# One graph layer's edge tiles on one core: which edges of part one go into the tile that both sorted parts share

## The reference

```python
edge_index = jnp.stack([src, dst])                 # sorted by dst
h = jnp.maximum(_layernorm(x, axis=-1), 0.0)
x = x + _L0_gnn_ref(h, edge_index, W, b)            # degree-normalised sum over edges, then a linear layer and relu
h = jnp.maximum(_layernorm(x, axis=-1), 0.0)
x = x + _L1_gnn_ref(h, edge_index, Wq, ...)

def _L1_gnn_ref(node_embeds, edge_index, ...):
    rows, cols = edge_index                         # rows = src, cols = dst
    q = node_embeds[rows] @ Wq.T + bq
    k, v = node_embeds[cols] @ Wk.T + bk, node_embeds[cols] @ Wv.T + bv      # 8 heads of 16
    exp_att = exp(clip(sum(q * k, per head) / 4, -10, 10))
    out = segment_sum(exp_att / (segment_sum(exp_att, rows)[rows] + 1e-8) * v, rows)
    return layernorm(out + node_embeds) * gamma + beta
```

## Time and profile before

| what | us |
|---|---|
| executions, lowest, median, highest | 2271.06, 2272.73, 2276.27 |
| profiled execution, span from first to last instruction | 2940.6 |
| setup and first tiles, 0 to 230 of the span | 230 |
| edge loop of the first layer, 230 to 1450 | 1220 |
| node rows and list of tiles, 1450 to 1575 | 125 |
| passes, 1575 to 2884 | 1309 |
| end | 56 |

### The profile page before, as it was taken

One profiled execution on the slowest core, in us unless ns is written; L12 is line 12 of the kernel. 1 busy time (PEld: TensorE's weight loads), 2 busy tenths in 40 slices (PEclk: granted clock), 3 DMA queues, 4 the chain that ended last, 5 costly groups with the idle time before them and its releaser, 6 DMA issues. The chain is left out here.

```text
span 2940.6 us, 44304 instructions
## 1 busy us (share of the span) xinstructions
PE 1840.2 (63%) x10257; PEld 1461.4 (50%) x10258; DVE 1874.7 (64%) x5089; ACT 1279.6 (44%) x3362; POOL 1551.0 (53%) x1594
## 2 busy tenths in 40 slices
PE   5323346767576676677776767676666676666662
PEld 4323334544344444344454656566556665656662
DVE  9858775655455755455775666666666666666666
ACT  8524345755465565556653323333223332322333
POOL 0256655665556565565434555545455555555544
PEclk7756667877778787878887888888888888888886
DMA  3211111111111111111116444445444544444453
GB/s 105 62 41 42 43 39 39 45 42 38 38 38 45 38 41 41 39 44 39 33 68 185 126 125 127 127 122 131 119 121 124 132 123 122 125 123 123 126 122 55
DMA packets 234145, 244.06 MB, mean 83 GB/s; under 512 B 32925, under 2 KB 195229, under 8 KB 233989
## 3 DMA queue, kind: packets, MB, share of 16 engines
q0 software_dynamic: 61136, 147.00, 18.5%
q1 hardware_dynamic: 142357, 81.55, 10.8%
q10 hardware_dynamic: 30624, 15.21, 2.2%
HBM read 225.01 MB, written 18.62 MB: 83 GB/s over the span
## 5 line engine op out<-in xcount | busy, mean ns | idle before, releaser
L303 POOL DMA_INDIRECT rows<-y_tab,idx x832 | 795.6, 956 | 589.8 <-issue 307.9
L1340 POOL DMA_INDIRECT x<-kv_tab,kv_idx x672 | 682.7, 1016 | 623.0 <-DVE msg L1392 403.9
L1563 PE MATMUL ps_kv<-kv_s,hot_low 128*128 x1362 | 406.0, 443 | 168.9 <-DVE hot_low L1364 90.0
L780 ACT ACTIVATE sort_v<-sort_t,staged,minus 128x128 f16<-128x128 f16 x914 | 360.7, 480 | 309.1 <-remote 243.1
L872 PE MATMUL ps_sort<-sort_hi,sort_v 128*128 128x496 f16 x1662 | 417.6, 403 | 117.3 <-issue 112.4
L619 DVE TENSOR_SCALAR sort_v<-iota_h,staged 128x128 f16<-128x128 f16 x748 | 243.2, 325 | 339.2 <-remote 269.0
L1550 PE MATMUL ps_m<-msg,x 128*128 128x136 f32 x1792 | 295.4, 315 | 243.4 <-DVE msg L1392 182.7
L830 PE MATMUL ps_sum<-rows,hot 128*128 128x128 f32 x1664 | 282.0, 323 | 250.3 <-issue 120.1
L1374 DVE TENSOR_TENSOR by_tile<-ps_q,x 128x512 f32<-128x512 f32 x224 | 154.5, 690 | 404.9 <-remote 257.4
L830 PEld LDWEIGHTS ps_sum<-rows,hot 128*128 128x128 f32 x1664 | 260.4, 235 | 271.8 <-issue 139.4
L1550 PEld LDWEIGHTS ps_m<-msg,x 128*128 128x128 f32 x1792 | 263.3, 219 | 263.1 <-issue 245.7
(11 more groups left out here) (290 smaller groups left out, 2072.2 us busy)
## 6 DMA issues: line engine op xcount, KB each, us to landing
weights<-tile_tab SPq DMA_DIRECT2D x114, 256.0 KB
x<-tile_tab SPq DMA_DIRECT2D x113, 256.0 KB
weights<-tile_tab ACTq DMA_DIRECT2D x58, 256.0 KB
rows<-y_tab,idx POOLq DMA_INDIRECT x832
x<-kv_tab,kv_idx POOLq DMA_INDIRECT x672
kv_tab<-kv_s SPq DMA_DIRECT2D x12, 512.0 KB
x<-x_in SPq DMA_DIRECT2D x1, 3328.0 KB, 13.3
out<-x SPq DMA_DIRECT2D x12, 256.0 KB
```

The costliest lines, as they stand in the source:

```text
L303: pool.indirect_dma_start(out=rows[:, k * SPAN + n, :], out_offset=None, in_=y_tab, in_offset=bass.IndirectOffsetOnAxis(ap=idx[:, k, n:n + ...
L780: last = nc.scalar.activation(to[:, k % 2, m, :], sort_t[:, k % 2, m, :], ACT.Relu, bias=staged[:, v, c:c + 1], scale=minus[:, v, c:c + 1])
L1340: pool.indirect_dma_start(out=rows[:, u, k, :], out_offset=None, in_=kv_tab, in_offset=bass.IndirectOffsetOnAxis(ap=idx[:, u, k:k + 1], ax ...
L1563: last = nc.tensor.matmul(ps_kv[:, k % 2, :], hot_low[:, w, k * P:(k + 1) * P], kv_s[:, ds(low + w, 1), :], start=w == 0, stop=w == WINDOW ...
```

## The change

It changes which `low` edges of part one go to the shared tile: the last ones instead of the first. Part one's whole tiles come first in the numbering and the shared tile last (so the high part of part one's numbers now names the block's first tile plus its t0 div 128 whole tiles), the lane isn't mirrored any more, and the column of part one's tiles is computed with NB instead of NB - 1. The number of tiles and of edges in each stays as it was. Three prefetches behind SP's loop of passes get another form of wait, which bounds the register's value from below and adds a no-operation.

```diff
@@ -440,15 +440,17 @@
                 then(nc.vector.tensor_copy(tiles[:, :, :], tiles_i[:, :, :]))
+                then(nc.vector.tensor_scalar(count[:, 0, :], tiles[:, 0, :], float(2 ** LIN), None, ALU.mult))
                 then(nc.vector.tensor_tensor_scan(flat(tend), flat(tiles), zeros_h[:, 0:2 * NB], 0.0, ALU.add, ALU.add))
...
-                nc.vector.tensor_scalar(count[:, 0, :], low, -1.0, float(P - 1), ALU.mult, ALU.add)
+                then(nc.vector.tensor_scalar(tiles[:, :, :], tiles[:, :, :], float(2 ** LIN + P), -float(MID * 2 ** LIN), ALU.mult, ALU.add))
+                then(nc.vector.tensor_tensor(tiles[:, 0, :], tiles[:, 0, :], count[:, 0, :], ALU.add))
+                nc.vector.memset(count[:, 0, :], -1.0)
                 then(nc.vector.tensor_scalar(count[:, 1, :], low, -1.0, None, ALU.add))
-                then(nc.vector.tensor_scalar(tiles[:, :, :], tiles[:, :, :], float(2 ** LIN + P), -float(MID * 2 ** LIN), ALU.mult, ALU.add))
                 then(nc.vector.tensor_tensor(tiles[:, :, :], tiles[:, :, :], count[:, :, :], ALU.add))
@@ -568,15 +570,16 @@
-                nc.vector.tensor_scalar(run[:, PARTS[0]], lane_of[:, PARTS[0]], -1.0, float(P - 1), ALU.mult, ALU.add)
-                nc.vector.tensor_copy(run[:, PARTS[1]], lane_of[:, PARTS[1]])
+                nc.vector.tensor_copy(run, lane_of)
...
-                then(nc.vector.scalar_tensor_tensor(out=pos, in0=tile_f, scalar=float(NB - 1), in1=sbk[:, :], op0=ALU.add, op1=ALU.subtract))
+                for part in range(2):
+                    then(nc.vector.scalar_tensor_tensor(out=pos[:, PARTS[part]], in0=tile_f[:, PARTS[part]], scalar=float(NB - part),
+                                                        in1=sbk[:, PARTS[part]], op0=ALU.add, op1=ALU.subtract))
@@ -1314,9 +1317,9 @@
-                def load_src(i, u):
+                def load_src(i, u, after=sp.wait_ge):
 
-                    sp.wait_ge(off_made, i * QUADS + u + 1)
+                    after(off_made, i * QUADS + u + 1)
@@ -1326,7 +1329,7 @@
                 for u in range(QUADS - 1):
-                    load_src(passes, u)
+                    load_src(passes, u, lambda semaphore, value: wait_positive(sp, semaphore, value))
```

## The result

The changed kernel takes 2239.12 us (median of 4, 2236.35 to 2244.36) beside 2274.50 for the kernel before (median of 4, 2271.06 to 2277.89): a ratio of 0.9851, interval 0.9834 to 0.9868, or 35.4 us less. The forecast was 2238 us.

A forecast was written before the change was run, and what follows sets the result against it. The prediction took a ring of DVE and PE to bound the passes, 23.2 us each when profiled. Two passes at 17.9 us saved 35.8, additions cost 0.5: 2272.7 - 35.3 = 2237.4, said as 2238 us; range 2225 to 2250.

The forecast's parts named there:

- The count: Tiles counted on the reference's inputs: narrow 184 to 206, fetched 670 to 648, so passes of the loop 56 to 54.
- The price of a pass: Stage 4's loop: a pass without the profiler takes 17.9 us, so two passes fewer save 35.8 us.
- the factor 0.773: Median 2272.73 us over the profiled span; scaled a pass from 23.2 to 17.9 us, the surplus laid to the profiler.
- The bounds: A pass's price lies between 15.3 us, four quads of the fastest stretch, and 23.2 us, the profiled mean.
- The ring of DVE and PE: Stage 4's passes: expand, products, scores, exponential, values, sums, next quad bound a pass; 23.2 us, DVE's own work 14.9.
- rival 1: Every pass runs like the fastest stretch, 15.3 us; 2242.6 us, chance 0.24; against it, POOL's 12 gathers already take 15.1.
- the weighed rule: Slow clock belongs to an idle TensorE; without the profiler PE stays nearer full clock and a pass costs the dense stretch's price.
- The additions: DVE's extra instructions in setup and behind the ranks: 0.65 us, taken as exposed, bounds 0 and 1.3.
- SP's waits: Three new-form waits behind SP's loop of passes: taken as 0, with 0.5 us at most.
- Dense passes: Without the profiler every pass runs like the fastest stretch, 15.3 us; 2242.6 us, chance 0.24.
- Dear passes: Surplus lies in stages 1 to 3, so a pass keeps 23.2 us; 2226.8 us, chance 0.06.
- The other three: 55 passes, 2255.3 us (0.04); timed inputs not those counted, about 2273 (0.02); slower instruction supply in passes, 2282 (0.04).

The follow-up runs named there:

- Narrow_of_two: Changed kernel with a narrow tile's limit set to a difference of 1 block instead of 2; 3160.40 us on chip B, 1.0743 of before.
- after: The changed kernel's own profiled execution, of the short kind, 2242.7 us long.
- after_again: The changed kernel itself, run again on chip C beside the kernel before; 2886.54 us, 0.9822 of before.
- waits_alone: Kernel before with only SP's three bounded waits added, on chip A; 2277.74 us beside 2277.71 for before, ratio 0.9996.
- nine_gathers_b: Changed kernel with three gathers in each fetched quad instead of four, on chip C; 2677.34 us, 209 us less than the changed kernel there.

## Why the prediction was right, point by point

**The count.** 854 tiles, 206 narrow, 648 fetched, 54 passes: shown by 648 gathers and 216 products. That there was no tile to spare did no harm. Narrow_of_two confirmed the method with 780 gathers. That most of the gain comes from part one's whole tiles and not from the shared ones is the count's statement, which the reference's inputs give again; no run separates the two, since they are one choice.

**The price of a pass.** The sum took 17.9 us, the runs show 16.65 (33.3 us for two, 35.8 forecast). It came out near because the factor 0.773 between median and span scaled every stage alike, and the true factors aren't far from it: 16.65 / 23.2 = 0.72 for the passes, and 0.79 for the edge loop: 1049 us from its first gather to its last in after, 1324 in after_again. POOL's gathers of the edge loop, after, then after_again (first and last start):

```profile
L303 POOL DMA_INDIRECT rows<-y_tab,idx x832: 940/947/1709, 120.3 to 1169.7; - x167
L303 POOL DMA_INDIRECT rows<-y_tab,idx x832: 938/944/1702, 120.6 to 1444.2; - x167
```

That the price came out near is so in part luck. The reason I gave for the factor, in the table and in the sum, was wrong: the surplus wasn't the profiler's. Before takes 2949 and 2943 us on chips B and C by its timed executions, and on chip A a profiled one takes no longer than the others (waits_alone: 2277.51 us profiled, median 2277.74). Had the median come from chip B or C, the price would have been the row's own 23.2. The bounds held: 15.3 and 23.2. The pass "again near 23 us" that the changed profile was to show was 16.6 in after and 23.2 in after_again.

**The bound.** The ring of DVE and PE as the bound was the step that failed. The mean pass was read from a trace in which POOL waits 404 us for DVE, so I set POOL aside; but nine_gathers_b shows that a pass gets shorter by its gathers' time in that very kind of execution (4.06 us for 3.96), and that DVE's idle time ahead of products, which I took for PE's work, is in large part a signal that comes long after that work is done. On the short kind the trace says it by itself: 12 gathers of 1.065 us and 12 gaps of 0.30 are 16.4 of 16.6 us. The number 15.1 us for them stood in rival 1, as a reason against it; a better lower bound than 15.3 comes from it with the mean of the earlier trace rows (1.016) in the place of the shortest pair: 12 x 1.316 = 15.8. This didn't touch the forecast, since a pass saved is saved whole whatever bounds it.

**The clock.** The granted clock in the passes is 0.99 in after and in waits_alone, and 0.85 in the earlier trace rows and 0.84 in after_again, where PE stands idle for up to 9 us. The Trainium skill, TensorE: Matmul & The Clock Gate, Part 1, has the slow clock as that of an idle TensorE; the rows agree. What the weighed rule foresaw, a dense pass at full clock, is what the short kind has, but at 16.6 us and not at PE's 15.3, as POOL is in the way.

**The additions.** 0.38 + 0.20 = 0.58 us measured, 0.65 forecast. The forecast's own terms, 0.5, 0.08 for the copy and twice 0.08 for the halves, are 0.74 and not 0.65; next to 35 us that changes nothing. SP's waits: nothing, within the interval of waits_alone.

**The rivals.** Dense passes was half right (clock and density yes, price no). Dear passes has the price of the long kind: on chip C, where a pass takes 23.2 us, the saving was 57 us, with an interval that takes in 46. But its reason, a surplus in stages 1 to 3, isn't what happened. The other three didn't happen. The sentence that a pass runs the same whatever its slots hold named its own weak place: its instructions are the same, its time isn't. An empty pass costs 23 to 25 us on chip A, where a full one costs 16.6. Here that has no effect on the forecast, since before has two empty fetched slots (672 for 670 tiles) and after none.

**What is left.** 54 passes are 864 slots for 854 tiles, and 53 would be 848: with tiles of 128 and one source block each no choice of the shared tile's edges brings a pass less. A faster kernel has to make the gathers of a pass cheaper or fewer, not the passes.

## What to carry to other kernels

Where a loop's count is computed from the data, count it on the inputs for both kernels before costing any instruction, check the count of before against the trace, and look how near it stands to the next step. The price of an iteration can then be bounded from the densest and the mean stretch, and two iterations taken away from the old kernel show it directly. Look whether the profiled execution and the timed ones are of the same kind before a factor between them is explained, and check that an experiment's edit reaches the data that it means to change.

## What the runs showed of the hardware

- One program has two kinds of time: before takes 2278 us on chip A and 2949 and 2943 on B and C. The mean length of a gather is no longer (1.02 us in after_again, 1.065 in after) and DVE's products take 0.69 us in both; the difference is idle time, on PE up to 9 us at once. In the passes much of it is a signal of PE that frees DVE and ACT, together, up to 7.6 us after the matmuls' end in after_again and within 0.8 us in after, and the long waits end as POOL's series of gathers does. What holds the signal up isn't shown.
- Gathers with one index in all lanes took three times the DMA engines' time per MB of ordinary ones (7.5 points against 2.4), and a pass without work took 23.2 us where one with work took 16.6. Those gathers read one row again and again; that this is what makes them dear is untested.
- An engine that was idle for 383 us waiting for another (POOL in after_again) still gave back its work one for one when it had less: three gathers fewer are 3.96 us with their gaps, and the pass got 4.06 us shorter.
